# Mamba-style mixer and top-2 expert layer on one core: expert results weighted by ScalarE and scattered by GpSimd to their token's row

## Chip, cores and metric

The kernel runs on one core of a Trainium2 chip, as one launch. The metric is the device time of that launch in microseconds (us), as the median of several runs.

## What is computed

The input `x` has 4 sequences of 1024 tokens with 256 features, 4096 tokens in all, in float32. Two layers follow each other, and each is added to its own input and normalized over the features:

```
x = layernorm(x + mixer(x))      # rms norm, in-projection, causal conv, state scan (16 states), gate, out-projection
x = layernorm(x + ffn(x))

ffn:  normed = rmsnorm(x) * norm_weight
      shared = relu(normed @ sw1 + sb1) @ sw2 + sb2                 # 256 -> 1024 -> 256
      probs  = sigmoid(normed @ router_w.T)                         # 8 experts
      w      = the 2 largest probs, divided by (their sum + 1e-6)
      routed = sum over the 2 chosen experts e of
               w_e * (relu(normed @ ew1[e] + eb1[e]) @ ew2[e] + eb2[e])
      return shared + routed
```

The kernel runs only the two chosen experts of a token: 8192 pairs of token and expert.

## The kernel before

`xall` holds all 4096 tokens on chip, as 32 groups of 128 rows. `TC` is 512 tokens, so there are `NT` = 8 tiles of `NSUB` = 4 groups. Each engine runs a program of its own, written out by hand in the blocks `gpsimd` (L390), `sync` (L504), `scalar` (L662), `vector` (L925) and `tensor` (L1263); they meet at semaphores. SyncE (SP) issues nearly all DMAs, in program order, from one queue; GpSimd (POOL) issues the indirect ones. Nothing reorders an engine's program, so an instruction that waits holds up all that is written behind it.

**Stage 1**, up to about 1073 us, is the mixer; the change does not touch it.

**Stage 2** goes over the 8 tiles. VectorE normalizes the tile (`norms`), TensorE multiplies it with the router and the shared expert (`up`, `down`), and VectorE picks two experts per token (`select`). For each of the 8 experts, `rows_dram` has a region of 4096 + 128 rows; `select` counts the tokens of each expert and so gives every pair a row in its region, `slots_now`. On POOL, `one_pass(k)` scatters the normalized rows of the tile there with 8 indirect DMAs of 128 rows (L474). The pair's row is also kept in `rows_of` (L1106) and its weight in `wts` (L1111).

**Between stages 2 and 3** VectorE makes the table of blocks (L1141 to L1174): the regions are cut in blocks of 128 rows, of which there are `NBLK` = 71 in every run, the largest number that can be needed; those that are not needed read spare rows of zeros. L1157 to L1171 turn each pair's row in its region into its row in the packed order of the blocks, `slots`. When the table is ready, SP loads the up-projection of the first two blocks (`load_up`, L602), writes 128 rows of zeros behind the last row of each expert in a loop of 8 (L608), waits for all scatters, loads `eb2_s` (L611) and then the rows of the first blocks (`load_block`, L616).

**Stage 3** is the loop over the 71 blocks, written so that two buffers alternate (`par`). For block i TensorE does `expert_up(i+1)` (L1469), `rows_T(i+2)` (L1457) and `expert_down(i)` (L1480). VectorE adds the biases: `add_b1` (L1185) and `add_b2` (L1194); the latter reads PSUM and writes `eo`, and frees PSUM for `expert_down(i+1)`. ScalarE applies the relu (L897) and copies the transposed rows (L889). SP issues `load_up(i+3)`, `load_block(i+4)` and `store_block(i)` (L620), which stores `eo` to the 128 rows of the block in `eo_dram`.

**Stage 4** waits until all blocks are stored (`stage3_over`), then goes over the 8 tiles as 4 sequences of two halves. VectorE hands POOL the rows of the tile (`hand_slots`, L1216), POOL gathers them with 8 indirect DMAs (L489), VectorE multiplies them by their weights and adds them to `xall` (L1224), takes mean and variance (L1230, L1234), ScalarE takes the root (L918), VectorE normalizes (L1241) into `fin`, and SP stores the tile (L652).

Of the kernel before, what the change touches and what calls it, by code (L numbers as in the profile page):

```python
# [47 lines left out]
def build(nc, x, norm_scale, w_in, conv_w, conv_b, A_log, D_skip, w_xproj, w_dt, b_dt, w_out,  # L48
# [36 lines left out]
    eo_dram = nc.dram_tensor("eo_dram", [NBLK * P, O], F32).ap()  # L85
# [16 lines left out]
    with ExitStack() as whole:  # L102
# [11 lines left out]
        slots = sb("slots", [P, TOPK, NSUBS], U32)  # L114
        rows_of = sb("rows_of", [P, TOPK, NSUBS])
        wts = sb("wts", [P, TOPK, NSUBS])
# [80 lines left out]
        slots_now = sb("slots_now", [P, TOPK, NSUB], U32)  # L197
        zero = sb("zero", [P, D])
# [4 lines left out]
        shift = sb("shift", [P, 3, E])  # L203
        shifts = sb("shifts", [P, TOPK * NSUBS])
# [10 lines left out]
        eo = sb("eo", [P, 2, O])  # L215
        eb2_s = sb("eb2_s", [P, E, O])
# [4 lines left out]
        slots4 = sb("slots4", [P, 2, TOPK, NSUB], U32)  # L221
        gat = sb("gat", [P, 2, NSUB, TOPK, D])
        st6f = sb("st6f", [P, 2, NSUB, 6])
        mvf = sb("mvf", [P, 2, NSUB, 2])
        scf = sb("scf", [P, 2, 2, NSUB])
        fin = sb("fin", [P, 2, NSUB, D])
# [81 lines left out]
        slots4_ready = sem("slots4_ready")  # L308
        gathered = [sem(f"gathered{i}") for i in range(2)]
        v4_ready = sem("v4_ready")  # L310
        sq4_ready = sem("sq4_ready")
        f_link = sem("f_link")
        fin_ready = sem("fin_ready")
        out_done = [sem(f"out_done{i}") for i in range(2)]
# [69 lines left out]
        LINKS2 = 31  # L384
        LINKS4 = 17
        W1_DMAS = 4
        SETUP2 = 9
# [3 lines left out]
        def _(pool):  # L391
# [69 lines left out]
            pool.wait_ge(s_c2, 7)  # L461
# [5 lines left out]
            def one_pass(k):  # L467
# [15 lines left out]
            def gather(b, half):  # L483

                pool.wait_ge(slots4_ready, b * HALVES + (half + 1))
                settled(pool)
                for s in range(NSUB):
                    for j in range(TOPK):
                        nc.gpsimd.indirect_dma_start(  # L489
                            out=gat[:, half, s, j, :], out_offset=None, in_=eo_dram,  # L490
                            in_offset=bass.IndirectOffsetOnAxis(ap=slots4[:, half, j, s:s + 1], axis=0)).then_inc(
                            gathered[half], 16)

            stage3_over(pool)
            def one_pass(b):
                for half in range(HALVES):
                    gather(b, half)

            one_pass(0)
            with pool.Fori(1, NB) as b:  # L500
                one_pass(b)
# [3 lines left out]
        def _(sp):  # L505
# [88 lines left out]
            for i in range(SPARE):  # L594
                sp.dma_start(rows_dram[E * REGION + i * P:E * REGION + (i + 1) * P, :], zero[:]).then_inc(zeroed, 16)
# [26 lines left out]
            assert NBLK % 2 == 1 and NBLK >= 9  # L622
# [6 lines left out]
            def one_pass(t):  # L629
                for par in range(2):  # L630
# [4 lines left out]
                    store_block(i, par)  # L635
# [7 lines left out]
            store_block(NBLK - 5, 0)  # L643
            load_up(NBLK - 1, 0)
            for i in range(NBLK - 4, NBLK):
# [881 lines left out]
```

## Time and profile before

| | before |
|---|---|
| median of 3 runs | 1999.08 us (1998.44 to 2000.59) |
| the profiled execution's own time | 1994.91 us |
| its span in the profile | 1993.0 us |
| PE busy | 1553.9 us (78% of the span) |
| DVE busy | 1172.8 us (59%) |
| POOL busy | 1004.7 us (50%) |
| ACT busy | 895.4 us (45%) |
| moved by DMA | 235.54 MB, mean 118 GB/s |

PE is TensorE's matmuls, PEld its weight loads, DVE VectorE, ACT ScalarE, POOL GpSimd, and SPq the DMAs that SyncE issues. Times in rows are us from the start of the span unless marked ns. Busy shares are means over stages with different limits, so the stages are read apart. An L number is a line of the kernel; one engine's idle time is followed by what ended it.

### The profile page before, as it was taken

The page shows a single profiled execution, that of the slowest core. Times are in us where ns is not written, and L with a number is a line of the kernel's source. Part 1 is how long each engine was busy: PE and PEld are TensorE (multiplying, and loading weights), DVE is VectorE, ACT ScalarE, POOL GpSimd, SP SyncE. Part 2 cuts the span into 40 slices and gives each one's busy share as a digit, 9 for nine tenths or more (in the row PEclk, how much of TensorE's full clock was granted, in tenths as well). Part 3 has the DMA queues.
Part 4 walks back from the last instruction along what each step waited for, and adds up shares of the span by engine and source line. Part 5 has one row for each costly group of instructions (what it writes and reads, how often), then busy time and mean ns, then how long its engine had stood idle before and what let it go on. Part 6 is the DMA issues. An engine that isn't in the chain of part 4 may idle for free.

```text
span 1993.0 us, 23250 instructions
## 1 busy us (share of the span) xinstructions
PE 1553.9 (78%) x6593; PEld 907.6 (46%) x6594; DVE 1172.8 (59%) x1853; ACT 895.4 (45%) x1666; POOL 1004.7 (50%) x431
## 2 busy tenths in 40 slices
PE   6486877868778688786563999994999999999900
PEld 2121221312213122231022666763999999999800
DVE  3298898888988889888893444422222222222256
ACT  4576676666766657666541343321222222222200
POOL 0598898988988988889881223120000000000075
PEclk9798888989989898797896999996999999999955
DMA  4643426444264442544424301014555555555344
GB/s 126 144 105 98 106 60 143 107 100 103 58 143 107 100 111 54 138 107 101 111 43 144 119 33 42 22 41 162 178 177 180 184 184 184 182 180 177 125 124 129
DMA packets 122137, 235.54 MB, mean 118 GB/s; under 512 B 15584, under 2 KB 53840, under 8 KB 121952
## 3 DMA queue, kind: packets, MB, share of 16 engines
q1 hardware_dynamic: 115936, 218.11, 38.9%
q0 software_dynamic: 6144, 16.79, 2.7%
q8 instruction: 22, 0.36, 0.1%
q14 instruction: 35, 0.29, 0.1%
HBM read 193.69 MB, written 41.16 MB: 118 GB/s over the span
## 4 chain that ended last, share of the span: by engine, by line
PE 46%; POOL 28%; DVE 9%; issue 7%; ACT 5%; DMA 3%; SPq 1%; POOLq 0%; DVEq 0%; ACTq 0%
POOL X L421 15%; PE psH L1469 13%; PE psP L1480 12%; PE psP L1391 6%; PE psH L1400 6%; POOL X L434 5%; DVE psH L973 4%; PE psP L1353 3%; POOL gat L489 2%; POOL ud L406 2%; POOL spe L403 2%; POOL spr L404 2%; POOL ud L409 2%; DVE X L984 1%; PE psA L1342 1%
## 5 line engine op out<-in xcount | busy, mean ns | idle before, releaser
L421 POOL TENSOR_TENSOR X<-rep,B 128x2048 f32<-128x2048 f32 x128 | 576.8, 4525 | 96.6 <-DMA rep<-ud_dram 64.3
L1342 PE MATMUL psA<-X,gsum 128*32 128x512 f32 x1024 | 330.9, 650 | 205.8 <-DVE X L984 188.7
L807 ACT ACTIVATE psH<-rep,A_q 128x512 f32<-128x512 f32 x512 | 350.1, 689 | 170.1 <-DVE X L984 157.1
L489 POOL DMA_INDIRECT gat<-eo_dram,slots x64 | 62.9, 982 | 583.1 <-DVE slots L1216 563.4
L973 DVE TENSOR_TENSOR_SCAN psH<-psH,X 128x512 f32<-128x512 f32 x192 | 233.2, 1220 | 84.3 <-POOL X L421 78.2
L1469 PEld LDWEIGHTS psH<-nTb,ew_s 128*128 128x128 f32 x2272 | 265.9, 193 | 3.6
L1469 PE MATMUL psH<-nTb,ew_s 128*128 128x128 f32 x2272 | 266.1, 276 | 0.0
L973 DVE TENSOR_TENSOR_SCAN psH<-psH,carry,X 128x512 f32<-128x512 f32 x192 | 243.9, 1278 | 33.8 <-POOL X L421 32.5
L1342 PEld LDWEIGHTS psA<-X,gsum 128*32 128x32 f32 x1024 | 45.5, 112 | 478.3 <-DVE X L984 403.1
L897 ACT ACTIVATE hT<-hT 128x512 f32<-128x512 f32 x142 | 89.4, 630 | 384.1 <-DVE hT L1185 384.1
L984 DVE TENSOR_TENSOR X<-psH,C 128x512 f32<-128x512 f32 x384 | 257.9, 672 | 0.0
L1480 PE MATMUL psP<-ew_s,hT 128*128 x1136 | 257.0, 379 | 0.7 <-DVE eo L1194 0.7
L1480 PEld LDWEIGHTS psP<-ew_s,hT 128*128 128x128 f32 x1136 | 210.3, 190 | 26.8 <-issue 1.1
L1185 DVE TENSOR_TENSOR hT<-psH,vecs 128x512 f32<-128x512 f32 x142 | 98.2, 691 | 196.5 <-PE psH L1469 196.5
L1290 PE MATMUL psP<-xnT,w_in_s 128*128 128x512 f32 x256 | 142.2, 684 | 34.3 <-ACT res L679 30.3
L474 POOL DMA_INDIRECT rows_dram<-nrm,slots_now x64 | 61.8, 966 | 197.4 <-DVE slots_now L1105 180.3
L434 POOL TENSOR_TENSOR X<-X,C 128x2048 f32<-128x2048 f32 x32 | 144.8, 4526 | 25.7 <-DVE X L973 14.4
L1194 DVE TENSOR_TENSOR eo<-psP,eb_s 128x256 f32<-128x256 f32 x71 | 30.1, 425 | 215.6 <-PE psP L1480 215.6
L1301 PE MATMUL psP<-xraw,convd 128*128 128x512 f32 x256 | 126.2, 640 | 18.4 <-ACT xraw L679 18.4
L1400 PE MATMUL psH<-sw_s,hT 128*128 128x256 f32 x512 | 121.5, 380 | 0.0
L1391 PE MATMUL psP<-nT,sw_s 128*128 128x512 f32 x256 | 121.4, 602 | 0.0
L1400 PEld LDWEIGHTS psH<-sw_s,hT 128*128 128x128 f32 x512 | 96.1, 190 | 32.9 <-issue 23.0
(173 smaller groups left out, 1614.5 us busy)
## 6 DMA issues: line engine op xcount, KB each, us to landing
ew_s<-in_L_ffn_ew_dram SPq DMA_DIRECT2D x79, 1024.0 KB, 4.9
rep<-ud_dram SPq DMA_DIRECT2D x128, 512.0 KB, 8.7
ud_dram<-ud SPq DMA_DIRECT2D x32, 512.0 KB, 2.6
xb<-rows_dram SPq DMA_DIRECT2D x71, 128.0 KB, 4.0
eo_dram<-eo SPq DMA_DIRECT2D x71, 128.0 KB, 1.7
B<-bc_dram SPq DMA_DIRECT2D x128, 64.0 KB, 6.3
C<-bc_dram SPq DMA_DIRECT2D x128, 64.0 KB, 7.2
out_dram<-fin SPq DMA_DIRECT2D x8, 512.0 KB, 3.5
```

Source lines behind the costliest of these rows:

```text
L421: nc.gpsimd.tensor_tensor(X[:, Q % NX], rep[:, g % 2, 1], B4[:, f:f + 1, :].broadcast_to([P, NR, TC]), ALU.mult).then_inc(bx_ready, 1)
L434: nc.gpsimd.tensor_tensor(X[:, Q % NX], X[:, Q % NX], C4[:, LAST:NF, :].broadcast_to([P, NR, TC]), ALU.mult).then_inc(cx_ready, 1)
L807: nc.scalar.activation(psH[:, r, :], rep[:, g % 2, 0, r, :], ACT.Exp, scale=A_q[:, c, r, f:f + 1]).then_inc(dA_ready, 1)
L973: nc.vector.tensor_tensor_scan(kept, psH[:, r, :], X[:, Q % NX, r, :], start, ALU.mult, ALU.add).then_inc(scan_done, 1)
L984: nc.vector.tensor_tensor(X[:, Q % NX, r, :], psH[:, r, :], C4[:, f, :], ALU.mult).then_inc(hc_ready, 1)
L1290: ins = nc.tensor.matmul(dst, w_in_s[:, d, m * P:(m + 1) * P], xnT[:, d, :], start=(d == 0), stop=(d == DC - 1))
L1301: ins = nc.tensor.matmul(dst, convd[:, j * CH + c, :], xraw[:, c % 2, j:j + TC], start=(j == 0), stop=(j == K - 1))
L1342: ins = nc.tensor.matmul(psA[r * GJ:(r + 1) * GJ, g % 2, :], gsum[:], X[:, Q % NX, r, :], start=False, stop=(f == NF - 1), skip_group_chec ...
L1391: ins = nc.tensor.matmul(psP[:, m % 2, :], sw1_s[:, d, m * P:(m + 1) * P], nT[:, d, :], start=(d == 0), stop=(d == DC - 1))
L1400: ins = nc.tensor.matmul(psY[:, s, 0:O], hT2[:, m % NH, s * P:(s + 1) * P], sw2_s[:, m, :], start=(m == 0), stop=(m == HC - 1))
L1469: ins = nc.tensor.matmul(psH[:, 2 * par + a, j * P:(j + 1) * P], ew1_s[:, par, d, m * P:(m + 1) * P], nTb[:, par, d, :], start=(d == 0), s ...
L1480: ins = nc.tensor.matmul(psP[:, 1, 0:O], hT[:, par, m, :], ew2_s[:, e, m, :], start=(m == 0), stop=(m == HC - 1))
```

## The change

In stage 2 each pair gets, beside its row, a record of two numbers: its weight, and its destination 1 + (0 or 4096) + token, that is, one row per token for the first choice and one for the second. POOL scatters these records to `meta_dram` with 8 more indirect DMAs per tile, of 128 records of 8 bytes, to the same rows as the data. SP zeroes `meta_dram` wherever it zeroes `rows_dram`, so that padding rows have weight 0 and destination row 0 of `con_dram`, a row that nobody reads. The table of packed rows (L1157 to L1171) goes.

In stage 3 SP loads each block's records (`load_meta`), DVE turns the destination into an integer and adds the second bias into `eb`, ACT multiplies by the weight into `eo` (`weigh`), and POOL scatters the 128 rows to `con_dram` (`hand_out`). A `hand_out` waits until the one before has landed. `store_block` goes.

In stage 4 SP loads all of `con_dram` in 16 plain DMAs of 512 KB into a buffer for all tiles; POOL adds the two rows of each token, DVE adds them to `xall` and takes the moments, ACT takes the root and normalizes in place, SP stores from `xall`.

```diff
-    eo_dram = nc.dram_tensor("eo_dram", [NBLK * P, O], F32).ap()
+    meta_dram = nc.dram_tensor("meta_dram", [ROWS, 2], F32).ap()
+    con_dram = nc.dram_tensor("con_dram", [1 + TOPK * T, O], F32).ap()
...
     # gpsimd, stage 2, one_pass(k), behind the 8 scatters of rows
+                pool.wait_ge(meta_ready, k + 1)
+                settled(pool)
+                for j in range(TOPK):
+                    for s in range(NSUB):
+                        nc.gpsimd.indirect_dma_start(
+                            out=meta_dram, out_offset=bass.IndirectOffsetOnAxis(ap=slots_now[:, j, s:s + 1], axis=0),
+                            in_=meta_now[:, j, s, :], in_offset=None).then_inc(meta_out, 16)
...
     # gpsimd, stage 3
+            def hand_out(i, par, turn):
+                after(pool, eo_out[1 - par], (turn + par) * 16)
+                pool.wait_ge(eo_ready, i + 1)
                 settled(pool)
+                nc.gpsimd.indirect_dma_start(
+                    out=con_dram, out_offset=bass.IndirectOffsetOnAxis(ap=dest[:, par, :], axis=0),
+                    in_=eo[:, par, :], in_offset=None).then_inc(eo_out[par], 16)
...
     # gpsimd, stage 4
+            for k in range(NT):
+                pool.wait_ge(con_here[k], TOPK * 16)
+                nc.gpsimd.tensor_tensor(con[:, k, 0], con[:, k, 0], con[:, k, 1], ALU.add).then_inc(both_ready, 1)
...
     # sync, the loop over the 8 experts before stage 3
                 sp.dma_start(rows_dram[ds(row, P), :], zero[:]).then_inc(zeroed, 16)
-            sp.wait_ge(zeroed, 16 * (SPARE + E))
+                sp.dma_start(meta_dram[ds(row, P), :], zero[:, 0:2]).then_inc(zeroed, 16)
+            sp.wait_ge(zeroed, 2 * 16 * (SPARE + E))
             sp.wait_ge(scattered, 16 * TOPK * NSUBS)
+            sp.wait_ge(meta_out, 16 * TOPK * NSUBS)
...
-            def store_block(i, par):
-                sp.wait_ge(eo_ready, i + 1)
-                sp.dma_start(eo_dram[ds(i * P, P), :], eo[:, par, :]).then_inc(eo_out[par], 16)
+            def load_meta(i, par, done):
+                row = sp.value_load(block_row[0:1, ds(i, 1)], min_val=0, max_val=ROWS - P)
+                after(sp, eo_ready, done)
+                sp.dma_start(mb[:, par, :], meta_dram[ds(row, P), :]).then_inc(mb_here[par], 16)
+            for i in range(2):
+                load_meta(i, i, 0)
...
     # scalar
+            def weigh(i, par):
+                act.wait_ge(eb_ready, i + 1)
+                nc.scalar.activation(eo[:, par, :], eb[:, par, :], ACT.Copy, scale=mb[:, par, 0:1]).then_inc(eo_ready, 1)
...
     # vector, select(k)
+                after(dve, meta_out, k * (16 * TOPK * NSUB))
                 nc.vector.tensor_copy(slots_now[:], picked[:, TOPK:]).then_inc(slots_ready, 1)
...
     # vector, add_b2(i)
+                dve.wait_ge(mb_here[par], turn * 16 + 16)
+                after(dve, eo_out[par], turn * 16)
+                nc.vector.tensor_copy(dest[:, par, :], mb[:, par, 1:2])
                 dve.wait_ge(B_done, i + 1)
-                after(dve, eo_out[par], turn * 16)
-                nc.vector.tensor_tensor(eo[:, par, :], psP[:, 1, 0:O], eb2_s[:, e, :], ALU.add).then_inc(eo_ready, 1)
+                nc.vector.tensor_tensor(eb[:, par, :], psP[:, 1, 0:O], eb2_s[:, e, :], ALU.add).then_inc(eb_ready, 1)
...
     # vector, stage 4: moments(k), then scales(k - 1)
+                dve.wait_ge(both_ready, k + 1)
+                link4.done(nc.vector.tensor_tensor(rows, rows, con[:, k, 0], ALU.add)).wait()
...
```

Two places of the programs show how it moves instructions. The first is SP in the loop of stage 3, one block, before (`ew_s` is the up-projection, `xb` the block's rows):

```order
L602 ISA [waits A_done]
L602 DMA ew_s<-in_L_ffn_ew_dram 128x2x1024
L615 ISA [waits T_done]
L615 TENSOR_LOAD block_row
L615 ISA x2
L616 ISA
L616 DMA xb<-rows_dram 128x256
L619 REGISTER_ALU
L620 ISA [waits eo_ready]
L620 DMA eo_dram<-eo 128x256
```

and the same place now:

```order
L620 ISA [waits A_done]
L620 DMA ew_s<-in_L_ffn_ew_dram 128x2x1024
L635 ISA [waits T_done]
L635 TENSOR_LOAD block_row
L635 ISA x2
L636 ISA
L636 DMA xb<-rows_dram 128x256
L639 REGISTER_ALU
L639 TENSOR_LOAD block_row
L639 ISA x2
L641 ISA [waits eo_ready]
L641 DMA mb<-meta_dram 128x2
```

The store of the block is gone from SP, and a load stands in its place behind the same semaphore, with a read of the block's row ahead of it. The second place is POOL from stage 3 to the end, before:

```order
L489 DMA gat<-eo_dram,slots 128x256 [waits slots4_ready,eo_out0,eo_out1]
L489 DMA gat<-eo_dram,slots 128x256 x7
L489 DMA gat<-eo_dram,slots 128x256 [waits slots4_ready]
L489 DMA gat<-eo_dram,slots 128x256 x7
L500 UNCONDITIONAL_BRANCH
```

and now:

```order
L501 DMA con_dram<-eo,dest 8193x256 [waits eo_ready]
L501 DMA con_dram<-eo,dest 8193x256 [waits eo_out0,eo_ready]
L510 UNCONDITIONAL_BRANCH
...
L501 DMA con_dram<-eo,dest 8193x256 [waits eo_out1,eo_ready]
L517 TENSOR_TENSOR con<-con 128x1024 [waits con_here0]
L517 TENSOR_TENSOR con<-con 128x1024 [waits con_here1]
```

The gathers of stage 4 are gone, one scatter per block stands in stage 3, each behind the landing of the one before, and eight adds of 128x1024 end the program.

## Rows read from the trace of the kernel before

**Rows 1.** The page's 40 equal slices of the span (49.8 us each): GB/s moved by DMA.
```profile
GB/s 126 144 105 98 106 60 143 107 100 103 58 143 107 100 111 54 138 107 101 111 43 144 119 33 42 22 41 162 178 177 180 184 184 184 182 180 177 125 124 129
```
**Rows 2.** The chain that ended last, its end: start, us, engine, tile, line.
```profile
1880.01 3.57 PE psH L1469 x32
...
1915.06 3.81 DMA gat<-eo_dram,slots
```
**Rows 3.** Timeline of one block of stage 3: start, us, engine, line [idle before].
```profile
1387.51 0.42 DVE L1194 TENSOR_TENSOR eo<-psP,eb_s 128x256 f32<-128x256 f32 x1 [2.98 <-PE psP L1480]
...
1390.03 0.63 ACT L897 ACTIVATE hT<-hT 128x512 f32<-128x512 f32 x1 [4.33 <-DVE hT L1185]
...
1394.74 0.42 DVE L1194 TENSOR_TENSOR eo<-psP,eb_s 128x256 f32<-128x256 f32 x1 [2.98 <-PE psP L1480]
```
**Rows 4.** Waits of SP's queue: line, for whom, us in total, times, longest.
```profile
SPq L620 <- DVE eo L1194: 187.3, 71, 6.9
SPq L602 <- PE psH L1469: 105.0, 69, 3.1
```
**Rows 5.** Timeline between stages 2 and 3.
```profile
1347.96 0.17 DVE L1157 TENSOR_TENSOR shift<-cum,nblk 128x8 f32<-128x8 f32 x1
1351.08 0.18 DVE L1172 CAST block_row<-bexp 1x71 int32<-1x71 f32 x1
1352.57 1.62 SPq L602 DMA_DIRECT2D ew_s<-in_L_ffn_ew_dram  x2
1355.13 11.43 SPq L608 DMA_DIRECT2D rows_dram<-zero  x8
1367.93 0.35 SPq L611 DMA_DIRECT2D eb_s<-in_L_ffn_eb_dram  x1
1369.05 7.44 SPq L616 DMA_DIRECT2D xb<-rows_dram  x4
1373.27 0.66 PE L1457 MATMUL psP<-ident,xb 128*128 128x128 f32 x2 [31.10 <-DMA xb<-rows_dram]
```
**Rows 6.** Timeline of stage 2: rows handed over, and POOL's last scatter.
```profile
1108.83 0.17 DVE L1105 CAST slots_now<-picked 128x8 uint32<-128x8 f32 x1
1139.49 0.17 DVE L1105 CAST slots_now<-picked 128x8 uint32<-128x8 f32 x1
1333.26 0.96 POOL L474 DMA_INDIRECT rows_dram<-nrm,slots_now  x1 [0.30 <-issue]
```
**Rows 7.** The page's DMA issues: count, KB each, median us to landing.
```profile
rows_dram<-nrm,slots_now POOLq DMA_INDIRECT x64, 2.4
gat<-eo_dram,slots POOLq DMA_INDIRECT x64, 2.8
out_dram<-fin SPq DMA_DIRECT2D x8, 512.0 KB, 3.5
```
**Rows 8.** Timeline from the last block to the first gather.
```profile
1891.61 0.42 DVE L1194 TENSOR_TENSOR eo<-psP,eb_s 128x256 f32<-128x256 f32 x1 [4.00 <-PE psP L1480]
1894.88 0.24 DVE L1216 COPY slots<-slots 128x8 uint32<-128x8 uint32 x2 [2.84 <-DMA eo_dram<-eo]
```
**Rows 9.** Window in which 8 MB of weights load in rows of 1 KB: last columns DMA share, GB/s.
```profile
1075.00:1100.00 25.00, 8.16 (x29) 6.44 (x30) 6.96 (x24) 6.77 (x16) 0.01 (x1) 0.55 1.03 339
```
**Rows 10.** Groups and single instructions: mean ns of one after the busy us.
```profile
L421 POOL TENSOR_TENSOR X<-rep,B 128x2048 f32<-128x2048 f32 x128 | 576.8, 4525 | 96.6 <-DMA rep<-ud_dram 64.3 <-PE psA L1342 32.3
L404 POOL TENSOR_TENSOR spr<-spr,ud 128x512 f32<-128x512 f32 x32 | 40.8, 1274 | 0.0
L846 ACT ACTIVATE junk<-xall 128x256 f32 x24 | 10.0, 416 | 2.3
1097.97 1.23 DVE L1073 TENSOR_TENSOR xall<-xall,sb_s 128x1024 f32<-128x1024 f32 x1 [6.71 <-ACT prob L861]
1985.56 1.41 DVE L1230 BATCH_NORM_STATS2 st6f<-xall 128x6 f32<-128x256 f32 x4 [0.15 <-DVE xall L1224]
1987.12 0.38 DVE L1234 BATCH_NORM_AGGREGATE mvf<-st6f 128x2 f32<-128x6 f32 x4 [0.15 <-DVE st6f L1230]
```

More of the change, by code:

```diff
@@ L307, in build @@
         eo_out = [sem(f"eo_out{i}") for i in range(2)]
-        slots4_ready = sem("slots4_ready")
-        gathered = [sem(f"gathered{i}") for i in range(2)]
+        meta_ready = sem("meta_ready")
+        meta_out = sem("meta_out")
+        mb_here = [sem(f"mb_here{i}") for i in range(2)]
+        eb_ready = sem("eb_ready")
+        con_here = [sem(f"con_here{k}") for k in range(NT)]
+        both_ready = sem("both_ready")
         v4_ready = sem("v4_ready")
@@ L312, in build @@
         f_link = sem("f_link")
+        nb_ready = sem("nb_ready")
         fin_ready = sem("fin_ready")
-        out_done = [sem(f"out_done{i}") for i in range(2)]
+        out_done = sem("out_done")
         block = whole.enter_context(nc.Block())
@@ L905, in one_pass @@
                     scale_rows(t * 2 + (par + 2), par)
+                    weigh(t * 2 + par, par)
             one_pass(0)
@@ L911, in _, with root4, finish4 @@
             scale_rows(NBLK - 1, 0)
+            weigh(NBLK - 3, 0)
             relu(NBLK - 1, 0)
-            def one_pass(b):
-                for half in range(HALVES):
-                    act.wait_ge(v4_ready, b * HALVES + (half + 1))
-                    nc.scalar.activation(scf[:, half, 1, :], scf[:, half, 0, :], ACT.Sqrt).then_inc(sq4_ready, 1)
-            one_pass(0)
-            with act.Fori(1, NB) as b:
-                one_pass(b)
+            weigh(NBLK - 2, 1)
+            weigh(NBLK - 1, 0)
+            def root4(k):
+                act.wait_ge(v4_ready, k + 1)
+                nc.scalar.activation(scf[:, k, 1, :], scf[:, k, 0, :], ACT.Sqrt).then_inc(sq4_ready, 1)
+            def finish4(k):
+                act.wait_ge(nb_ready, k + 1)
+                for s in range(NSUB):
+                    row = xall[:, k * NSUB + s, :]
+                    ins = nc.scalar.activation(row, row, ACT.Identity, scale=scf[:, k, 2, s:s + 1],
+                                               bias=scf[:, k, 3, s:s + 1])
+                ins.then_inc(fin_ready, 1)
+            for k in range(NT):
+                root4(k)
+                if k:
+                    finish4(k - 1)
+            finish4(NT - 1)
         @block.vector
@@ L1233, in tile4 @@
                 for s in range(NSUB):
-                    link4.done(nc.vector.bn_aggr(out=mvf[:, half, s, :], in_=st6f[:, half, s, :]))
-                link4.wait()
-                nc.vector.tensor_scalar(scf[:, half, 0, :], mvf[:, half, :, 1], 1e-5, None, ALU.add).then_inc(v4_ready, 1)
-                dve.wait_ge(sq4_ready, b * HALVES + (half + 1))
-                link4.done(nc.vector.reciprocal(scf[:, half, 1, :], scf[:, half, 1, :])).wait()
-                after(dve, out_done[half], b * 16)
@@ L1255, in _, with scales @@
-            one_pass(0)
-            with dve.Fori(1, NB - 1) as b:
-                one_pass(b)
-            link4.start((NB - 1) * (HALVES * LINKS4))
-            for half in range(HALVES):
-                tile4(NB - 1, half)
+                    ins = nc.vector.bn_aggr(out=mvf[:, k, s, :], in_=st6f[:, k, s, :])
+                link4.done(ins).wait()
+                nc.vector.tensor_scalar(scf[:, k, 0, :], mvf[:, k, :, 1], 1e-5, None, ALU.add).then_inc(v4_ready, 1)
+            def scales(k):
+                dve.wait_ge(sq4_ready, k + 1)
+                link4.done(nc.vector.reciprocal(scf[:, k, 2, :], scf[:, k, 1, :])).wait()
+                nc.vector.scalar_tensor_tensor(out=scf[:, k, 3, :], in0=mvf[:, k, :, 0], scalar=-1.0,
+                                               in1=scf[:, k, 2, :], op0=ALU.mult, op1=ALU.mult).then_inc(nb_ready, 1)
@@ L1263, in _ @@
+            for k in range(NT):
+                moments(k)
+                if k:
+                    scales(k - 1)
+            scales(NT - 1)
         @block.tensor
```

139 lines of the change are left out of this document (46 added, 93 removed).

## The prediction

> **What bounds the kernel now.** I read the slices first, then the end of the chain of waits, then timelines of the three places that the change touches. The slices show 177 to 184 GB/s through stage 3 and only 124 to 129 in the last three, so stage 4 is not short of bandwidth [rows 1]. The chain ends with TensorE's products of stage 3, one after the other, and then steps to the gathers of POOL [rows 2], which has nothing to do in stage 3. A block of stage 3 takes 7.24 us (1394.74 - 1387.51), of which up is 3.57 and down with the transposes the rest [rows 2, 3]. Everything else there is cover: DVE sits idle 2.98 us before each second bias, ACT about 1.6 us between that bias (over at 1387.93) and its next relu (1390.03, after 4.33 idle) [rows 3]. So the change can win only in stage 4 and between stages 2 and 3; stage 3 must stay at 7.24 us per block.
>
> **Stage 4 before.** It runs from 1894.88, when DVE hands the first rows over [rows 8], to the end of the span at 1993.0: 98.1 us for 64 gathers, at 98.1 / 64 = 1.53 us each; an issue and its gap alone take 1.26 (0.96 + 0.30 for the scatters of stage 2 [rows 6]). This is issue-bound work, not bandwidth: 64 x 128 KB plus 4 MB out.
>
> **Stage 4 after.** 16 plain loads of 512 KB are 8.39 MB. Loads with the same 1 KB rows ran at 339 GB/s with the DMA engines full [rows 9], so the 1.05 MB of a tile take 3.1 us. Count from t0, when the last scatter has landed. First tile here: some 2 us for start and landing (the 128 KB store of the last block was here after 2.85 - 0.4 [rows 8]) + 3.1 = 5.1. POOL adds two 128x1024 tiles: between 1274 ns for 512 and 4525 ns for 2048 the straight line gives 2.36 us [rows 10]. DVE per tile: add 1.23, wait 0.15, statistics 1.41, wait 0.15, aggregate 0.38, epsilon 0.2 = 3.5, and 0.4 for reciprocal and bias of the tile before = 3.9 [rows 10]. ACT: four rows x 0.416 + root 0.2 = 1.9 [rows 10], POOL 2.36, loads 3.1: all below 3.9, so **DVE sets the pace**. Stage 4 is 5.1 + 2.4 + 7 x 3.9 + 3.5 = 38.3, then root and scales 0.7, ACT 1.7, last store 3.5 [rows 7] = **44.2 us**. The stores, 4.2 MB more, fit: 12.6 MB at 0.339 take 37 us, and all but the last tile can go while DVE works.
>
> **A price that no row shows** is two adds at once: POOL's tile add beside DVE's, each with both inputs on chip. From below nothing: DVE's add beside stage 1's POOL adds is never of this kind. From above, each of the 8 DVE adds waits for one whole POOL add, 8 x 2.36 = 19 us. POOL is busy 2.36 of every 3.1 us only while tiles still come, up to t0 + 30. Walking the two programs through with "whoever comes second waits", DVE's third, fourth and fifth add wait some 2 us each, and the end moves by 6 us. I take 5, near the lower end, since the adds after t0 + 30 are alone. The Trainium skill (SBUF — State Buffer, "Who interferes with whom") says that a VectorE instruction with two SBUF inputs and a GpSimd one that reads SBUF exclude each other for the whole instruction. By that rule the sum would have 6 here, without it 0; no row of this case decides.
>
> Stage 4 goes from 98.1 to 49: **-49**.
>
> **Between stages 2 and 3.** L1157 to L1171 go: 1351.08 - 1347.96 = **-3.1** [rows 5], on the path, since SP waits for the table. SP's zeroing loop takes 11.43 us for 8, 1.59 per turn [rows 5]; a second DMA in a turn costs at least its issue of 0.35 and at most the 1.24 from one load_up to the next with its table read (1.62 - 0.38): 2.8 to 9.9 us for eight. The row is read already, so I take 0.5 each: **+4.0**. Two load_meta now stand ahead of the first load_block, 2 x 1.2 us by the same distance; but that load lands at 1373.2, behind the 1 MB of eb2 issued at 1367.93, so most of this is covered [rows 5]: +0.5 (0 to 2.4).
>
> **Stage 2.** POOL's work per tile doubles to 16 x 1.26 = 20.2 us. The next tile's rows may be written only when the records have landed: 1.0 + 20.2 + 2.4 = 23.6 us after the hand-over, against a tile time of 30.66 (1139.49 - 1108.83) [rows 6, 7]. Cover 7 us: 0. The last records: 1334.2 + 10.4 + 2.4 = 1347, before SP asks at 1364: 0. The Trainium skill (DMA: Bandwidth & Descriptors, "Specifications") says that below 512 B the engine does a read-modify-write; it gives no price for 8 B. The sum stays unless an issue takes over 2.1 us.
>
> **Stage 3, per block.** SP: the record's load waits for the same semaphore as the store did, which now comes after ACT, 0.55 us later, and reads the table first (0.8 us). SP had 187.3 / 71 = 2.6 us of waiting there and 105.0 / 69 = 1.5 before load_up [rows 4]: 0. Behind it load_up is what could hurt; it has 1.0 us left, then the 6 us that its weights come early. DVE: an integer copy of 0.17 in the 2.98 idle. PSUM is freed by DVE as before, so TensorE waits for nobody new. ACT: weigh 0.42 fits before the relu. POOL: issue to landing 2.4 to 2.8 [rows 7] against 7.24: 0. If one of these covers went, a full turn would be paid 71 times.
>
> **Last block.** Before, bias over at 1892.03, stored at 1894.88: 2.85 us [rows 8]. After: weigh 0.5 + scatter 2.8 = 3.3: **+0.5**. Padding rows, and whole blocks at the end, all go to row 0 of con_dram; their price is between 0 and a full period, 7 us, for the last one: I take **+1**, near a normal landing.
>
> **Sum:** -49 - 3.1 + 4.0 + 0.5 + 0.5 + 1 = **-46** (all open costs at their lower ends give -54, all at their upper ends -18). The profiled execution's 1994.91 becomes 1949; it lies 4.2 below the median shown, so against 1999.08 I forecast **1953 us**, with a span near 1947.
>
> **Rivals.**
> - *The adds pass each other* in stage 4: 5 us less, and with the lower end of the zeroing cost 1947. For it: no row shows one add held up by another; against it: none shows two such adds side by side either. 25%.
> - *Stage 4 is held up at every tile*: each of DVE's adds waits for a whole one of POOL, 19 us in the place of 5, or the stores lie behind the loads in the one queue: 1953 + 14 = 1967, to 1970. For it: all transfers there are SP's; against it: 37 us of traffic in 44. 15%.
> - *The serial scatter sets the block's period* (slower): hand_out(i) waits for the landing of i - 1, add_b2(i) for that of i - 2, and TensorE's next down for add_b2. From a scatter of 7.2 us on, the excess is paid 71 times; 46 us are lost at 7.9 us, and at 8.5 the time is 1953 + 71 x 1.25 = 2042. Against it: indirect DMAs of the same size land in 2.4 and 2.8 [rows 7]; for it: these rows ran without 180 GB/s beside them. 4%.
> - *Nothing moves*: stage 4's gain is real only if its path was POOL; the chain says so. A wait in stage 3 worth 0.65 us a block would cancel it. 1%.
>
> **Numbers.** The forecast has 55%. The range of 8 in 10 takes the first rival and most of the second in: 1944 to 1970. A change of 0.2% (4 us) is about what can be told here. Faster 0.95, same 0.01, slower 0.04.
>
> **What would show it.** Right: a period of 7.24 between TensorE's products in stage 3; POOL's scatters about 1 us each, landing below 3; first L1457 of stage 3 near 1374 to 1375; stage 4 in 45 to 50 us with DVE tiles 3.9 apart, some of them 6 where L517 of POOL runs; DMA near 340 GB/s for 25 us. Wrong: TensorE waiting in stage 3 for L922, the record's load or the weights; a last scatter that lands late; ACT or the stores ending stage 4 more than 5 us behind DVE.

## The result, and the profile after

The changed kernel takes **1953.56 us** (median of 4 runs, 1950.79 to 1954.7) where the kernel before takes 1999.84 on the same chip (4 runs, 1998.44 to 2001.54): a ratio of **0.9764** (95% interval 0.9749 to 0.9778). The forecast was 1953.0. The profiled execution took 1953.10 us with a span of 1951.3, 41.7 less than the 1993.0 of before.

First the way into stage 3: a timeline of the changed kernel, the answer to [rows 5]. Each row has its start and its length in us, the engine and the line, and in brackets the engine's idle time before it.

```profile
1345.09 1.22 DVE L1157 TENSOR_TENSOR xall<-xall,psH 128x1024 f32<-128x1024 f32 x1 [17.85 <-PE psH L1402]
...
1351.27 0.19 DVE L1198 TENSOR_SCALAR block_exp<-bexp 1x71 int32<-1x71 f32 x1
...
1352.48 1.62 SPq L620 DMA_DIRECT2D ew_s<-in_L_ffn_ew_dram  x2
...
1367.15 0.33 SPq L626 DMA_DIRECT2D rows_dram<-zero  x1
...
1369.09 0.34 SPq L626 DMA_DIRECT2D rows_dram<-zero  x1
1369.61 0.33 SPq L627 DMA_DIRECT2D meta_dram<-zero  x1
1373.64 0.35 SPq L631 DMA_DIRECT2D eb_s<-in_L_ffn_eb_dram  x1
1375.10 1.47 SPq L641 DMA_DIRECT2D mb<-meta_dram  x2
1377.33 5.31 SPq L636 DMA_DIRECT2D xb<-rows_dram  x4
1379.45 0.66 PE L1459 MATMUL psP<-ident,xb 128*128 128x128 f32 x2 [34.40 <-DMA xb<-rows_dram]
```

From the last shared-expert add to the finished table it is now 6.37 us (1351.46 - 1345.09), before 9.26: -2.9. A turn of the zeroing loop takes 1.94 us (1369.09 - 1367.15) against 1.59 [rows 5], the whole loop 3.5 more (14.9 in the place of 11.43). SP then waits 3.4 us for the zeros to land where it waited 1.1: +2.3. From the bias table's load to the first transpose it is 5.81, before 5.34: +0.5.

Now the last block and stage 4, by the same view:

```profile
1898.24 0.42 DVE L1220 TENSOR_TENSOR eb<-psP,eb_s 128x256 f32<-128x256 f32 x1 [3.55 <-PE psP L1482]
1898.70 0.51 ACT L922 ACTIVATE eo<-eb,mb 128x256 f32<-128x256 f32 x1 [3.92 <-DVE eb L1220]
...
1899.98 0.96 POOL L501 DMA_INDIRECT con_dram<-eo,dest  x1 [3.46 <-ACT eo L922]
1903.11 2.03 SPq L675 DMA_DIRECT2D con<-con_dram  x4
...
1911.20 1.23 DVE L1243 TENSOR_TENSOR xall<-xall,con 128x1024 f32<-128x1024 f32 x1 [12.54 <-POOL con L517]
...
1914.66 1.23 DVE L1243 TENSOR_TENSOR xall<-xall,con 128x1024 f32<-128x1024 f32 x1
...
1918.23 2.18 DVE L1255 SCALAR_TENSOR_TENSOR scf<-mvf,scf 128x4 f32<-128x4 f32 x1
1920.33 1.21 DVE L1243 TENSOR_TENSOR xall<-xall,con 128x1024 f32<-128x1024 f32 x1
...
1923.89 2.34 DVE L1255 SCALAR_TENSOR_TENSOR scf<-mvf,scf 128x4 f32<-128x4 f32 x1
1926.15 1.21 DVE L1243 TENSOR_TENSOR xall<-xall,con 128x1024 f32<-128x1024 f32 x1
...
1929.71 0.16 DVE L1255 SCALAR_TENSOR_TENSOR scf<-mvf,scf 128x4 f32<-128x4 f32 x1
```

And POOL in the same stretch, from its own timeline:

```profile
1908.83 2.34 POOL L517 TENSOR_TENSOR con<-con 128x1024 f32<-128x1024 f32 x1 [7.88 <-DMA con<-con_dram]
1911.83 2.80 POOL L517 TENSOR_TENSOR con<-con 128x1024 f32<-128x1024 f32 x1 [0.66 <-DMA con<-con_dram]
1914.83 5.55 POOL L517 TENSOR_TENSOR con<-con 128x1024 f32<-128x1024 f32 x2 [0.20 <-DMA con<-con_dram]
1920.86 5.35 POOL L517 TENSOR_TENSOR con<-con 128x1024 f32<-128x1024 f32 x2 [0.47 <-DMA con<-con_dram]
```

From the start of the last second bias to the first load of stage 4 it is 4.87 us (1903.11 - 1898.24), where it was 3.27 (1894.88 - 1891.61) [rows 8]: +1.6. Stage 4 is 48.2 us (1951.3 - 1903.11) where it was 98.1: **-49.9**. A tile costs DVE 3.46 us (1914.66 - 1911.20) where nothing is in its way and 5.7 to 5.8 where something is. What is in its way is small: the product for the bias, 128x4, takes 0.16 us alone and 2.18 and 2.34 beside a whole add of POOL. An add of POOL alone takes 2.34; where DVE's add was there first it takes 2.7 or 2.8, and once 3.37: that one starts at 1929.84, 0.05 us behind an add of DVE (1929.79, 1.22 us), and its length is the two together less 0.2.

The sum of the differences is +2.8 (the last shared-expert add starts that much later; 2.2 of it is there at the end of stage 1, which the change doesn't touch) - 2.9 (the table) + 6.3 (from the table to the first transpose) + 0.5 (stage 3, 518.79 us from the first transposes to the last bias, before 518.34) + 1.6 - 49.9 = -41.7, up to rounding.

### The profile page after: what moved, and what is told of

It is laid out like the page before. It is cut to its first block, busy times and chain, and to the rows that moved or that the text cites. A ratio compares the mean times of both kernels' runs of the same rounds, so it can differ in the third digit from the quotient of the medians.

```text
span 1951.3 us, 23869 instructions
## 1 busy us (share of the span) xinstructions
PE 1558.1 (80%) x6593; PEld 908.9 (47%) x6594; DVE 1155.9 (59%) x1828; ACT 947.3 (49%) x1769; POOL 1094.2 (56%) x511
## 4 chain that ended last, share of the span: by engine, by line
PE 46%; POOL 28%; DVE 11%; issue 7%; ACT 4%; DMA 2%; SPq 1%; POOLq 0%; ACTq 0%; DVEq 0%
POOL X L425 16%; PE psH L1471 13%; PE psP L1482 13%; PE psP L1393 6%; PE psH L1402 6%; POOL X L438 5%; DVE psH L1011 4%; PE psP L1355 3%; DVE X L1022 2%; POOL ud L410 2%; POOL ud L413 2%; POOL spe L407 2%; POOL spr L408 2%; PE psA L1344 1%; DVE X L1011 1%
## 5 line engine op out<-in xcount | busy, mean ns | idle before, releaser
L501 POOL DMA_INDIRECT con_dram<-eo,dest x71 | 68.0, 957 | 483.4 <-ACT eo L922 483.4
L1220 DVE TENSOR_TENSOR eb<-psP,eb_s 128x256 f32<-128x256 f32 x71 | 30.1, 425 | 193.4 <-PE psP L1482 193.4
L922 ACT ACTIVATE eo<-eb,mb 128x256 f32<-128x256 f32 x71 | 36.1, 509 | 162.9 <-DVE eb L1220 162.9
```

## The experiments

Twelve kernels on three chips (the result above is from a run of its own): experiments 1 to 4 on chip A, 5 to 8 and 11 to 12 on chip B, 9 and 10 on chip C. The kernel before has medians of 2000.96 (A), 2005.37 and 2005.35 (B) and 2006.01 us (C). Experiments 1 to 8 were to say what stage 4, the entry to stage 3 and the new scatters cost; from 5 on a larger question came up.

**1. Plain loads in the kernel before** (leaves the gathering out).

```diff
-                for s in range(NSUB):
-                    for j in range(TOPK):
-                        nc.gpsimd.indirect_dma_start(
...
+                nc.gpsimd.dma_start(gat[:, half].rearrange("p s j d -> p (s j) d"),
+                                    eo_dram[0:TOPK * NSUB * P, :].rearrange("(n p) d -> p n d", p=P)).then_inc(
+                    gathered[half], 16)
```

> The kernel before, with the 8 gathers of a tile replaced by one plain load of 1024 fixed rows on the same queue (so the gathering is left out, and stage 4 adds wrong rows). If stage 4 was bound by the issue of 64 indirect DMAs at 1.26 us each, a tile falls from about 11 us to VectorE's own 8.4 us, stage 4 from 98 to about 5 + 8 x 8.4 + 4 = 76 us, and the time from 1999.8 to about 1978. If it was bound by moving the rows, it stays within 3 us of 1999.8.

Measured: 1975.06 us, 0.9871 (0.9849 to 0.9893). DVE's weighted sums, from its timeline:

```profile
1903.11 3.38 DVE L1221 SCALAR_TENSOR_TENSOR xall<-gat,wts,xall 128x256 f32<-128x256 f32 x8 [7.00 <-DMA gat<-eo_dram]
1910.63 3.38 DVE L1221 SCALAR_TENSOR_TENSOR xall<-gat,wts,xall 128x256 f32<-128x256 f32 x8
```

The same bytes in one DMA a tile: 7.5 us for a tile, all of it DVE's work, and at most 8.4 where DVE still waits for a load, and stage 4 is 72.4 us instead of 98.1. So stage 4 before was held by the 64 gathers and not by the number of bytes; the other half of the gain is DVE's lighter program. The edit also reads rows that lie in order where the gathers read scattered ones. That the issues were the limit, and not the scattered reading, the trace of before shows: they run from 1896.02 to 1980.2, 1.31 us each, where an issue and its gap alone are 1.26.

**2. DVE makes both adds**, POOL none.

```diff
-                dve.wait_ge(both_ready, k + 1)
-                link4.done(nc.vector.tensor_tensor(rows, rows, con[:, k, 0], ALU.add)).wait()
+                dve.wait_ge(con_here[k], TOPK * 16)
+                for j in range(TOPK):
+                    link4.done(nc.vector.tensor_tensor(rows, rows, con[:, k, j], ALU.add)).wait()
```

> The changed kernel, with VectorE making both adds of a tile and GpSimd none. If the 2.2 and 2.3 us that the 0.16 us scale product on 128x4 lasts twice are waits for GpSimd's add, no such product lasts over 0.3 us here; a tile takes 3.5 + 1.25 = 4.7 us on VectorE, it starts 2.3 us earlier, and stage 4 lasts 48 us as now, the time 1953 to 1955. If they come from the transfers, two or three products still last 2 us and stage 4 lasts 52.

Measured: 1955.15 us, 0.9769 (0.9744 to 0.9794). With nothing of POOL's beside it no product takes over 0.17:

```profile
1917.62 0.16 DVE L1252 SCALAR_TENSOR_TENSOR scf<-mvf,scf 128x4 f32<-128x4 f32 x1
1917.70 2.48 DVE L1240 TENSOR_TENSOR xall<-xall,con 128x1024 f32<-128x1024 f32 x2
...
1922.42 2.47 DVE L1240 TENSOR_TENSOR xall<-xall,con 128x1024 f32<-128x1024 f32 x2
```

Every tile costs 4.72 us (1922.42 - 1917.70), and stage 4 is 50.4, where I expected 48. POOL's help is worth 2 us of stage 4, no more: 8 adds of 1.2 us saved, some 5 us given back in collisions, 2.4 for its first add.

**3. The product's second input in PSUM.**

```diff
+                inv = psA[:, 0, k * NSUB:(k + 1) * NSUB]
...
+                link4.done(nc.vector.reciprocal(inv, scf[:, k, 1, :])).wait()
...
-                                               in1=scf[:, k, 2, :], op0=ALU.mult, op1=ALU.mult).then_inc(nb_ready, 1)
+                                               in1=inv, op0=ALU.mult, op1=ALU.mult).then_inc(nb_ready, 1)
```

> The changed kernel, with the scale product's second input in PSUM in the place of SBUF (one 0.17 us reciprocal more per tile). If two SBUF inputs on VectorE and a reading GpSimd instruction exclude each other, the product stays at 0.2 us beside GpSimd's adds, only the 128x1024 adds still meet them, and stage 4 falls from 48.2 to about 44 us, the time to about 1949.5. If any VectorE instruction beside a GpSimd add is held up, the product still lasts over 2 us twice and nothing is won.

Measured: 1952.68 us, 0.9754 (0.9730 to 0.9777), which can't be told from no gain. DVE's timeline says why:

```profile
1919.38 0.16 DVE L1257 SCALAR_TENSOR_TENSOR scf<-mvf,psA 128x4 f32<-128x4 f32 x1
1919.46 3.10 DVE L1243 TENSOR_TENSOR xall<-xall,con 128x1024 f32<-128x1024 f32 x1
...
1924.97 0.16 DVE L1257 SCALAR_TENSOR_TENSOR scf<-mvf,psA 128x4 f32<-128x4 f32 x1
1925.04 3.33 DVE L1243 TENSOR_TENSOR xall<-xall,con 128x1024 f32<-128x1024 f32 x1
```

The product passes (0.16 beside POOL's add), and the add behind it, 1.22 alone, pays instead. The instruction with two inputs in SBUF waits, whatever its size; one with an input in PSUM does not. My error was to take the instruction that waited for the cause of the wait.

**4. The record table zeroed early in stage 2**, none of it in the loop.

```diff
-                sp.dma_start(meta_dram[ds(row, P), :], zero[:, 0:2]).then_inc(zeroed, 16)
-            sp.wait_ge(zeroed, 2 * 16 * (SPARE + E))
+            sp.wait_ge(zeroed, 16 * (SPARE + E))
...
+                sp.dma_start(flat[:, at:at + n], zero[:, 0:n]).then_inc(meta_zeroed, 16)
```

> The changed kernel, with all of meta_dram zeroed in three DMAs early in stage 2, ahead of the first scatter of records, and no zeroing of it in SyncE's loop. If the loop's second DMA and the landing of the 8-byte writes are what the entry of stage 3 pays, a turn falls from 1.95 to 1.59 us or below, the wait behind the loop from 3.4 to 1.1 us, TensorE's first transpose of stage 3 comes 5.5 to 6 us earlier, the time is about 1948. If the entry waits for the last scatter of records instead, nothing moves.

Measured: 1949.08 us, 0.9738 (0.9713 to 0.9763), 4.5 us less than in the result, on another chip; the two ratios' intervals overlap, so the timeline has to show the gain. SP's:

```profile
1355.05 11.37 SPq L633 DMA_DIRECT2D rows_dram<-zero  x8
1367.79 0.35 SPq L637 DMA_DIRECT2D eb_s<-in_L_ffn_eb_dram  x1
```

The bias table is loaded 5.85 us earlier than at 1373.64: the 3.5 of the loop and 2.3 of the wait for landing. Both belong to the second zeroing DMA.

**5 and 6. The scatter of a block made two and three times in a row**, each waited for.

```diff
+                for r in range(1):
+                    nc.gpsimd.indirect_dma_start(
+                        out=con_dram, out_offset=bass.IndirectOffsetOnAxis(ap=dest[:, par, :], axis=0),
+                        in_=eo[:, par, :], in_offset=None).then_inc(again, 16)
+                    pool.wait_ge(again, i * 16 + (r + 1) * 16)
+                    settled(pool)
```

> The changed kernel, with each block's scatter done twice, the second after the first has landed. One scatter takes 2.4 us to land (3.1 at the last block) and starts 0.8 us after ScalarE's weighing, so two take about 0.8 + 2 x 2.7 = 6.2 us of the 7.24 us of a block. If the slack is what the profile says, stage 3 keeps 7.24 us a block and only the last block pays, 1956 us. If a scatter's true cost is more than it seems, the period grows already here.

> The same with three scatters in series, about 3 x 2.7 = 8.1 us, over the block's 7.24. If the serial scatter becomes the bound where the forecast's rival put it, the period of stage 3 grows to 8.1 to 8.6 us, GpSimd never waits for ScalarE, and the time is 2010 to 2050 us. If the two buffers hide it, it stays near 1960.

Measured: 2118.12 us (1.0568, 1.0545 to 1.0591) and 2331.03 us (1.163, 1.1605 to 1.1655), far off. POOL's scatters in stage 3, all of them, first and last start, of the one and of the other kernel:

```profile
L508 POOL DMA_INDIRECT con_dram<-eo,dest x71: 957/957/967, 1477.2 to 2065.3; - x71
```

```profile
L508 POOL DMA_INDIRECT con_dram<-eo,dest x71: 958/958/962, 1465.7 to 2278.4; - x71
```

A block takes 8.40 us with two scatters (588.1 / 70) and 11.61 with three (812.7 / 70), where with one it is 7.20 by the same reckoning (1395.9 to 1900.0). So the third costs 3.2 us. In both kernels POOL waits at nearly every block for its own scatters to land, and for ScalarE only once, so from two scatters on the rival "the serial scatter sets the block's period" is real. How far one alone was from it no run shows. The straight line back gives a period of 5.2 us (8.40 - 3.2), with 2 us to go. But in experiment 5 the second scatter lands 4.1 us after its issue in the median and the first 2.6, where the single one lands in 2.4: at 1706.93 the second starts beside 1 MB of weights that SP issued at 1705.34 and that take 4.9 us. By a landing of 2.4 and 0.8 to the next start one alone needs 3.2 us, with 4 to go. Both are estimates. The longer stage 3 is +84 and +309 us. The rest of the excess wasn't in stage 3, and I first saw it in the next two.

**7. Padding rows sent to 128 different rows** instead of all to row 0.

```diff
-    con_dram = nc.dram_tensor("con_dram", [1 + TOPK * T, O], F32).ap()
+    con_dram = nc.dram_tensor("con_dram", [P + TOPK * T, O], F32).ap()
...
-                sp.dma_start(meta_dram[ds(row, P), :], zero[:, 0:2]).then_inc(zeroed, 16)
+                sp.dma_start(meta_dram[ds(row, P), :], blank[:]).then_inc(zeroed, 16)
```

> The changed kernel, with 128 unread rows at the head of con_dram in the place of one, so that the padding rows of a block go to rows of their own. If the last scatter lands in 3.1 us in the place of 2.4 because all its 128 rows go to one row, it lands in 2.4 to 2.5 here and the time is 0.6 us less. If 3.1 is what any scatter takes there, nothing moves. Either way less than the runs can tell; the landing in the profile decides.

Measured: 2023.77 us, 1.0093 (1.0061 to 1.0125). The small effect is there: from the last scatter's issue to the first load of stage 4 it is 2.4 us (1973.5 to 1975.9), where all to row 0 took 3.1 (1899.98 to 1903.11, and 1965.8 to 1968.9 on this chip, in experiment 11). But the kernel is 70 us slower than the changed kernel of the result.

**8. The records scattered twice**, to a second table too.

```diff
+                        nc.gpsimd.indirect_dma_start(
+                            out=meta2_dram, out_offset=bass.IndirectOffsetOnAxis(ap=slots_now[:, j, s:s + 1], axis=0),
+                            in_=meta_now[:, j, s, :], in_offset=None).then_inc(meta_out, 16)
```

> The changed kernel, with each record scattered to a second table as well: 24 issues a tile in stage 2, 24 x 1.26 = 30.3 us, with start and landing 33.8 us from one hand-over to the next against TensorE's 30.66. If the cover was the 7 us of the forecast, a tile of stage 2 takes 33.5 to 34 us from the second on and the time grows by 20 to 24 us, to 1975. If GpSimd's issues have more cover, it stays at 1954.

Measured: 2131.19 us, 1.0633 (1.0610 to 1.0656). The eight hand-overs of stage 2 (DVE writes `slots_now` for POOL), of experiment 7 and of this one:

```profile
L1148 DVE CAST slots_now<-picked x8: 171/172/174, 1113.5 to 1396.3; 128x8 uint32<-128x8 f32 x8
```

```profile
L1148 DVE CAST slots_now<-picked x8: 171/172/172, 1111.9 to 1486.3; 128x8 uint32<-128x8 f32 x8
```

From the first hand-over to the last it is seven tiles. A tile of stage 2 takes 40.4 us (282.8 / 7) in the one and 53.5 in the other; in the changed kernel of the result it took 30.66 (1111.7 to 1326.3), as before. Experiment 7 changes nothing of stage 2 but a constant in the destinations and a table made at the start.

**9 and 10. The planner's table ahead of the last shared-expert add** (9), and with it experiments 3 and 4 and the first rows loaded ahead of the bias table (10).

```diff
                 if not last:
                     norms(k + 1)
                     assert link.n == LINKS2, link.n
-                add_shared(k)
+                    add_shared(k)
...
+            add_shared(NT - 1)
```

> The changed kernel, with the table of blocks made ahead of the last add of stage 2 (VectorE waits 17.85 us for TensorE there) and SyncE's zeroing begun at once; the first rows of stage 3 are loaded when that add is done. If the entry of stage 3 is SyncE's chain behind the table, it shifts by the 18 us up to TensorE's end of stage 2: first transpose at about 1379 - 18 = 1361 us, the time 1935 to 1938. If something else holds it (the scatter of the last records lands near 1352), it comes at 1358 or later all the same.

> The early table, meta_dram zeroed early, the first rows loaded ahead of eb2 and of the records, and the scale product from PSUM. The zeroing loop (11.4 us) then ends at about 1348 and the first transpose comes at 1353 to 1355 us, 25 us earlier than in the changed kernel; stage 4 stays at 48 us, since the run before showed that the wait only moves to the next add. 1928 to 1931 us. If the records' landing bounds the entry, 1933 or more.

Measured, on the third chip: 2001.61 us (0.9984, 0.9970 to 0.9999) and 1995.97 us (0.9936, 0.9915 to 0.9958). The part they aim at did shrink: from the last hand-over to the first transpose of stage 3 it is 44.0 us (1381.8 to 1425.8) and 35.9 (1392.7 to 1428.6), in place of some 35 and 28 by what I expected, where the changed kernel has 53.1 and the kernel before 49.9. Stage 2 took it all back: tiles of 38.9 and 40.0 us. In experiment 9 the zeroing loop now runs beside the last record scatters (the last is issued at 1403.66), and SP's timeline shows it held up too:

```profile
1391.65 0.39 SPq L626 DMA_DIRECT2D rows_dram<-zero  x1
...
1395.79 0.00 SPq L626 DMA_DIRECT2D rows_dram<-zero  x1
...
1401.47 0.00 SPq L626 DMA_DIRECT2D rows_dram<-zero  x1
...
1407.30 0.34 SPq L626 DMA_DIRECT2D rows_dram<-zero  x1
...
1409.26 0.34 SPq L626 DMA_DIRECT2D rows_dram<-zero  x1
```

4.1, 5.7 and 5.8 us a turn, and 1.96 from 1407.30 on, 3.6 us after the last issue. No run on another chip has this loop beside record scatters.

**11 and 12. The changed kernel without an edit, and the record as part of the row**, on one chip. In 12 the row that is scattered anyway has 258 columns, with weight and destination in the last two; sixteen scatters a tile become eight, the second table and its zeroing go, and it has the early table of experiment 9 and the first rows loaded first.

```diff
-    rows_dram = nc.dram_tensor("rows_dram", [ROWS, D], F32).ap()
-    meta_dram = nc.dram_tensor("meta_dram", [ROWS, 2], F32).ap()
+    rows_dram = nc.dram_tensor("rows_dram", [ROWS, D + 2], F32).ap()
...
-                            in_=nrm[:, s, :], in_offset=None).then_inc(scattered, 16)
+                            in_=nrm[:, j, s, :], in_offset=None).then_inc(scattered, 16)
...
-                nc.vector.tensor_tensor(meta_now[:, :, :, 0], picked[:, 0:TOPK],
+                nc.vector.tensor_tensor(nrm[:, :, :, D], picked[:, 0:TOPK],
...
+                nc.vector.tensor_copy(nrm[:, :, :, D + 1], dest_no[:]).then_inc(meta_ready, 1)
...
-                sp.dma_start(mb[:, par, :], meta_dram[ds(row, P), :]).then_inc(mb_here[par], 16)
+                sp.dma_start(mb[:, par, :], rows_dram[ds(row, P), D:D + 2]).then_inc(mb_here[par], 16)
```

> The changed kernel once more, without an edit. In all six variants of the last two batches stage 2 took 39 to 53 us a tile instead of 30.66, though most of them leave stage 2 as it is, and in each the same place lost the time: ScalarE's hT step waited 5 to 6 us twice a tile while the eight 8-byte record scatters were under way (15.4 us with the records written twice). Theory 'the chip': the 8-byte scatters do this on some chips, whatever else the kernel holds. Then on a chip of that kind this kernel has tiles of 39 to 41 us and a ratio to the kernel before of 0.99 to 1.00; on a chip of the first kind tiles of 30.66 us and a ratio of 0.976. Rival 'the edits': something in the variants did it; then tiles of 30.66 us and 0.976 on any chip.

> The record (weight and row number) rides as two more columns of the row that is scattered anyway: 1032-byte rows, eight scatters a tile in place of sixteen, no second table to zero, the record loads of the expert stage read two columns of the rows. The planner's table goes ahead of the last shared-expert add, and the first two blocks' rows are loaded ahead of the bias table and the records. On a chip where the changed kernel has tiles of 30.66 us: the entry to stage 3 loses its 4.0 us of second zeroing DMAs, 2.3 us of landing and some 11 us of table and loads, so 1953.6 - 17 = about 1936 (1930 to 1943), ratio 0.967. Theory 'the 8-byte scatters': the same time, and tiles of 30.66 us, also on a chip where the changed kernel has tiles of 39 to 41 us, with no ScalarE wait over 3.2 us on hT in stage 2. Rival 'any scatter beside ScalarE's work': tiles stay above 35 us there. VectorE's normalized rows are written twice (4 x 0.3 us more a tile), which PE's 3 us of cover before the transposes hides.

Measured: the changed kernel **2017.22 us**, ratio **1.0051** (1.0034 to 1.0067): on this chip it is slower than before. With the record in the row **1927.14 us**, ratio **0.9609** (0.9593 to 0.9625). The same program, then, gains 2.4% on one chip and loses 0.5% on another, and the edits are cleared. Where ScalarE waits from 1110 to 1330, within stage 2, by the list of waits (us in total, times, the longest): the changed kernel of the result, the same on chip B, and the record in the row on chip B.

```profile
ACT hT L891 <- PE psP L1393: 115.6, 57, 3.2
```

```profile
ACT hT L891 <- remote: 63.8, 10, 9.9
ACT hT L891 <- PE psP L1393: 49.9, 22, 3.4
```

```profile
ACT hT L881 <- PE psP L1384: 114.3, 56, 3.2
```

"remote" is the profile's word for a release by no instruction that it shows. The word alone proves little: on chips B and C the traces have no landings for the scatters of stage 2, not even in 12, where nothing is held up. What counts is when TensorE ends and when ScalarE starts. One such wait from near by, in timelines of ScalarE, of TensorE and of POOL of experiment 11:

```profile
1205.19 0.19 ACT L867 ACTIVATION_READ_ACCUMULATOR junk<-xall 128x1 f32 x1
1214.92 0.69 ACT L891 ACTIVATE hT<-psP,vecs 128x512 f32<-128x512 f32 x1 [9.54 <-remote]
```

```profile
1203.93 1.88 PE L1393 MATMUL psP<-nT,sw_s 128*128 128x512 f32 x4
1205.65 1.89 PE L1402 MATMUL psH<-sw_s,hT 128*128 128x256 f32 x8
1207.37 1.88 PE L1393 MATMUL psP<-nT,sw_s 128*128 128x512 f32 x4
1215.66 3.78 PE L1402 MATMUL psH<-sw_s,hT 128*128 128x256 f32 x8 [6.41 <-ACT hT L891]
```

```profile
1205.19 0.96 POOL L487 DMA_INDIRECT meta_dram<-meta_now,slots_now  x1 [0.30 <-issue]
...
1214.03 0.96 POOL L487 DMA_INDIRECT meta_dram<-meta_now,slots_now  x1 [0.30 <-issue]
```

TensorE's products that ScalarE waits for end at 1205.8. Elsewhere ScalarE starts 0.04 us behind them; here it starts at 1214.92. The wait lies inside POOL's eight record scatters (first issue 1205.19, last 1214.03), and TensorE then runs dry for 6.4 us. POOL itself keeps its 1.26 us per issue, and the DMA engines are 6% busy. During the eight row scatters just ahead of them (1195.03 to 1204.9) ScalarE starts on time. It is so in all seven kernels with separate records on B and C: each of ScalarE's waits over 3.5 us ahead of this relu (`hT`) in stage 2, up to two a tile, overlaps a batch of record scatters. Their longest is 17.5 us where the records are written twice. With the record in the row, stage 2 has its 30.66 us again (1139.34 to 1170.00 to 1200.66) on the very chip where the changed kernel has 39.1 (1113.0 to 1386.4, in 7). This refutes the rival "any scatter beside ScalarE's work".

Stage 2 from the first hand-over to the last, of the kernel of the result and of experiment 11 (stretch, its length, then busy us of PE, PEld, DVE, ACT and POOL, the granted clock as a share of full speed, DMA share, GB/s):

```profile
1111.70:1326.30 214.60, 214.60 (x869) 149.11 (x868) 92.83 (x350) 82.27 (x161) 108.18 (x112) 1.00 0.11 36
```

```profile
1113.00:1386.40 273.40, 238.17 (x869) 163.03 (x868) 92.62 (x350) 81.77 (x161) 108.06 (x112) 0.91 0.09 28
```

TensorE, which never rests in the one, is idle for 35.2 us in the other, and its same 869 products take 23.6 us more at a lower granted clock. After the first hold, in which it was dry for 6.1 us, the clock is 0.51 from 1137 to 1150, the lower of its two levels (1.2 GHz), and eight products on `hT` take 3.78 us in place of 1.89. So 40% of the loss is the clock that follows the waits.

The profiled executions of 11 and 12 are 93.8 us apart in span (2017.1 and 1923.3), the medians 90. What of the 93.8 is whose? Ahead of the first hand-over 4.3 (1113.0 against 1108.7). Stage 2: 273.4 - 214.6 = 58.8. The entry, from the last hand-over to the first transpose: 59.3 (1386.4 to 1445.7) against 28.1 (1323.3 to 1351.4): 31.2. Stages 3 and 4 -0.5. Against the changed kernel on the chip of the result, the entry alone is 25.0 shorter; the finished table is 19.2 nearer to the last hand-over (5.8 us, there 25.0), the zeroing loop 3.3 shorter, 2.5 are in the landing and the loads. 1953.56 - 25.0 = 1928.6, and 1927.14 was measured, on a chip on which the kernel before takes 5.5 us more, so the agreement is rough. I had expected 1936 (1930 to 1943): the table's move was priced at less than 11 us, and is 19.

## Why the prediction was right, and where not

- **The time**: forecast 1953, median 1953.56. That it fits within 1 us is luck in part. Between the two profiled executions, which all these terms are read from, it is -41.7 where -46 was forecast; the profiled execution of before happens to be 4.2 us below its median, and that of the changed kernel lies at its median. The terms left out are the +2.8 that is there before the last shared-expert add, which I can't lay to any step of the change, and the landing of the zeros, below.
- **Stage 4 before is issue-bound** and its end falls with the gathers: shown by experiment 1 and by the 64 issues in a row, 84 of the 98.1 us. The 1.53 us each of the forecast had the start and the last tile in it. Forecast -49, measured -49.9.
- **Its terms**: first tile 5.1, measured 5.7 (1903.11 to 1908.83); POOL's add 2.36, measured 2.34; DVE's tile 3.9, measured 3.46, since the waits of 0.15 that I counted aren't there (the statistics start 0.03 us behind the add) and the small instructions start 0.08 to 0.12 apart where I took 0.2 each; the end 9.4, measured 10.9 (1940.37 to the end). Errors of +0.6, -3.1 and +1.5 us cancel in part.
- **Colliding adds**: I took 5 us, the walk-through gave 6. Measured: eight starts of DVE's add span 29.17 us (1911.20 to 1940.37) where 7 x 3.46 = 24.2 would do, so 4.9. By the rule of the Trainium skill (SBUF — State Buffer, "Who interferes with whom") 6 would have stood in the sum, without it 0; the trace agrees with the rule, by the products of 2.18 and 2.34 us and by POOL's add of 3.37. What I had not seen is who waits: not the third to fifth add, but the 128x4 product ahead of it, and if that is let through, the add again (experiment 3).
- **The table** -3.1, measured -2.9. **The zeroing loop** +4.0, measured +3.5. **Loads at the entry** +0.5, measured +0.5. **Left out**: the landing of the zeros, +2.3, as experiment 4 shows; I looked at what SP issues and not at what it then waits for.
- **Stage 3, 0 per block**: measured 0 (518.79 against 518.34 us in all). Experiments 5 and 6 put the cover of the scatter at 2 to 4 us per block. The rival's point was put at a scatter of 7.2 us, and one needs 3.2 to 5.2 with its waits. That two in a row would still fit, as I expected, was wrong. The forecast's 1.6 us between the second bias and the relu on ACT are 2.1 by its own rows (1390.03 - 1387.93); `weigh` takes 0.51 of them and fits.
- **Last block** +0.5 and padding +1: measured +1.6 together, of which all rows going to one row is 0.7.
- **Stage 2, 0**: this is the step that held only on the chip of the result and on A. The reckoning was about POOL's queue and the landing: 23.6 us of 30.66. It is right as far as it goes: in experiment 11 DVE doesn't wait for the records' landing either. But I asked only what waits for the records; on chips B and C ScalarE is held up, which waits for nothing of theirs. I had named the 8 bytes as the unusual thing about these scatters and then priced them by their issue. The Trainium skill (DMA: Bandwidth & Descriptors, "Specifications") says that below 512 B the engine does a read-modify-write; no run here shows whether that is what holds ScalarE up. Measured on B: 8.4 us a tile, 58.8 in all, more than all of the gain in stage 4. Where the records are written twice it is 23 us a tile; where they ride in the row, 0.

So the number was right on the chip of the result, and it would have been 64 us off on chip B.

## What to carry to other kernels

A few bytes that belong to a row that is moved anyway should ride in that row: a separate scatter of 8-byte pieces costs as many issues as the rows themselves, needs its own zeroing and landing, and on two of the chips here it came with waits of engines that have nothing to do with it. Measure a kernel with an unusual traffic pattern on more than one chip before its gain is believed. And where an instruction waits for a shared resource, ask who is next in the line: letting it through may only hand the wait on.

## What the runs showed of the hardware that I had not expected

- Beside the 8-byte indirect scatters other engines are held up on two of the chips. On chip B ScalarE starts 9.1 us behind the end of TensorE's product (1205.8 and 1214.92), and on chip C a turn of SyncE's loop takes 5.8 us in place of 1.96. On chip A and on the one of the result stage 2 shows none of it: 30.66 us a tile in all four kernels with record scatters. All six variants on B and C show it, and on B the changed kernel itself.
- That it comes with the records is shown by 8 (doubled: 53.5 us a tile) and 12 (gone: 30.66). What about them does it isn't shown. They are 8 bytes each, and they are also a second batch of eight scatters right behind the first, and 12 takes both away; no run makes sixteen scatters of whole rows one after the other. What in the chips, or in where the tables lie in their memory, makes the difference stays open, as does the path by which the engines are held up (none was tried).
- A DVE instruction of 128x4 with both inputs in SBUF takes 0.16 us alone and up to 2.34 beside a POOL add of 2.34; where DVE's add came first, it is POOL's that takes longer, 2.69 to 3.37. The wait stands in the instruction's own length and not in the idle time before it.
- 128 rows of 1 KB scattered to one and the same row land 3.1 us after the issue, to different rows 2.4.
